# A ConvNet-and-experts layer: convolution by banded kernel matrices on TensorE, experts only on their own rows

## The chip, the cores and the metric

The kernel runs on one core of a Trainium2 chip. The metric is the device time of one execution in microseconds, median of the runs. All data is float32; matmuls are fp32 or f32r (float32 in TensorE's reduced form).

## The reference, cut to what matters

```python
r = relu((LN(x) @ w_reduce - mean) * gamma / sqrt(var + BN_EPS) + beta)   # 4x56x56, 128 -> 32
kgen = (r @ w_span + b_span).reshape(B, H, W, 16, 49)       # a 7x7 kernel per pixel and group
conv = einsum('bhwgk,bhwkgc->bhwgc', kgen, patches(LN(x)))  # 16 groups of 8 channels
t = x + conv
probs = softmax(LN(t) @ gate_w + gate_b)                    # 8 experts
cw = top two of probs, the others 0
out = t + sum_e cw[:, e] * (gelu(LN(t) @ W1[e] + b1[e]) @ W2[e] + b2[e])   # 128 -> 256 -> 128
```

There are 12,544 rows (pixels). Every expert is summed, but six of the eight weights of a row are zero.

## The kernel before

A row group is four image rows of two of the four images: 112 partitions (56 columns x 2 images) by four rows. There are 28 such groups (`q` and `bo`), each with eight steps `u` (an image row and half of the seven horizontal taps). All engines run the same loop `slot(q, bo)` in step order; later stages of earlier groups lie beside the convolution of the present one (`LAG_IN` = 14 steps later the first expert product, `LAG_OUT` 15, `LAG_WEIGH` 16, `LAG_ADD` 17).

Convolution: `kernels` makes on TensorE the kernels of 112 pixels, 4 or 3 horizontal taps at a time (L952). `products` on VectorE multiplies them with the normalised pixels over 3584 or 2688 elements (L744). POOL (`folds`, L434, L440) and, in two steps of eight, VectorE (`thin`, L750) add taps pairwise. `gather_taps` adds what is left on TensorE, by transposes that accumulate in one PSUM bank (L973). Two product tiles may lie between VectorE and TensorE.

Experts: for every group all eight experts are computed on all 448 rows. `expert_in` is three f32r matmuls of 448 columns for each half of the hidden layer (L1037 to L1039), `gelus` on ScalarE (L631), `expert_out` 8 fp32 matmuls (L1050), `weigh` on ScalarE scales by the row's weight `cw` (L621) and `add_expert` on VectorE sums (L764). SP only loads and stores; POOL also has the pow of the normalisations (L408) and the low part of the features `rT` (L421). Nothing is sorted and no DMA is indirect.

## Time and profile before

| | |
|---|---|
| runs | 1304.63, 1304.9, 1310.25 us; median 1304.9 |
| profiled execution, span of its core | 1302.3 us |
| VectorE, TensorE, POOL, ScalarE busy | 95%, 89%, 78%, 72% |
| mean granted TensorE clock | 0.954 |

The profiled execution's own time is its span and what lies around it; the three runs' median is 2.6 us over the span. A row of the profile gives line, engine, operation, output <- inputs with their tile names, and the shapes. An fp32 matmul that is no transpose leaves two records, each with its own weight load (engine PEld). Idle time in brackets names what ended it.

### The profile page before, as it was taken

The page shows a single profiled execution, that of the slowest core. Times are in us where ns is not written, and L with a number is a line of the kernel's source. Part 1 is how long each engine was busy: PE and PEld are TensorE (multiplying, and loading weights), DVE is VectorE, ACT ScalarE, POOL GpSimd, SP SyncE. Part 2 cuts the span into 40 slices and gives each one's busy share as a digit, 9 for nine tenths or more (in the row PEclk, how much of TensorE's full clock was granted, in tenths as well). Part 3 has the DMA queues.
Part 4 walks back from the last instruction along what each step waited for, and adds up shares of the span by engine and source line. Part 5 has one row for each costly group of instructions (what it writes and reads, how often), then busy time and mean ns, then how long its engine had stood idle before and what let it go on. Part 6 is the DMA issues. An engine that isn't in the chain of part 4 may idle for free. (4 is left out here: it accounts for less than half of the span.)

```text
span 1302.3 us, 27229 instructions
## 1 busy us (share of the span) xinstructions
PE 1154.1 (89%) x8857; PEld 1081.4 (83%) x8857; DVE 1237.1 (95%) x1222; ACT 941.2 (72%) x2975; POOL 1016.6 (78%) x558
## 2 busy tenths in 40 slices
PE   3999988999898889989888988898898889998987
PEld 3898888888788878889887888798888878888987
DVE  7789999999999999999999999999999999999942
ACT  3478877776777778777767777787777677667676
POOL 3248888988898898889888988988898889888830
PEclk9899999989999999889999999999999999899999
DMA  4100111011001101100110011011001100000000
GB/s 120 30 22 2 29 30 30 2 28 28 11 18 28 29 0 29 29 25 4 29 28 8 21 28 29 0 29 29 22 7 29 28 8 15 22 15 2 15 8 15
DMA packets 50007, 28.74 MB, mean 22 GB/s; under 512 B 6106, under 2 KB 46906, under 8 KB 49916
## 3 DMA queue, kind: packets, MB, share of 16 engines
q1 hardware_dynamic: 49892, 27.78, 7.8%
q8 instruction: 26, 0.43, 0.1%
q14 instruction: 65, 0.53, 0.1%
q10 hardware_dynamic: 24, 0.00, 0.0%
HBM read 15.38 MB, written 6.42 MB: 17 GB/s over the span
## 5 line engine op out<-in xcount | busy, mean ns | idle before, releaser
L744 DVE TENSOR_TENSOR prod<-kg,xn 112x3584 f32<-112x3584 f32 x224 | 762.0, 3414 | 9.2 <-PE kg L952 7.8
L434 POOL TENSOR_TENSOR prod<-prod 112x1536 f32<-112x1536 f32 x208 | 656.3, 3155 | 144.6 <-DVE prod L744 124.4
L1050 PE MATMUL y<-w_t,hT 128*112 128x128 f32 x3584 | 446.2, 279 | 0.0
L1050 PEld LDWEIGHTS y<-w_t,hT 128*112 128x112 f32 x3584 | 426.6, 184 | 2.1
L621 ACT ACTIVATE weighed<-y,cw 112x128 f32<-112x128 f32 x784 | 224.4, 373 | 140.1 <-DVE cw L837 104.0
L973 PE MATMUL conv<-ident,prod 112*128 112x112 f32 x2472 | 303.0, 276 | 0.0
L973 PEld LDWEIGHTS conv<-ident,prod 112*128 112x128 f32 x2472 | 279.8, 151 | 22.9 <-issue 12.7
L631 ACT ACTIVATE hT<-h,b_t 128x448 f32<-128x448 f32 x448 | 266.9, 657 | 43.0 <-PE h L1039 42.5
L440 POOL TENSOR_TENSOR prod<-prod 112x512 f32<-112x512 f32 (+1 forms) x182 | 249.3, 1370 | 14.3
L764 DVE TENSOR_TENSOR acc<-weighed,acc 112x512 f32<-112x512 f32 x168 | 180.7, 1076 | 18.8 <-ACT weighed L621 18.8
L1037 PE MATMUL h<-tn_hi,w_hi 128*128 128x448 f32 x448 | 182.2, 407 | 16.4 <-ACT hT L631 16.4
L1039 PE MATMUL h<-tn_hi,w_lo 128*128 128x448 f32 x448 | 167.8, 374 | 0.0
L1038 PE MATMUL h<-tn_lo,w_hi 128*128 128x448 f32 x448 | 167.2, 373 | 0.0
L952 PE MATMUL kg<-wk,rT 98*112 98x112 f32 x784 | 123.6, 275 | 22.4 <-DVE prod L744 19.5
L952 PEld LDWEIGHTS kg<-wk,rT 98*112 98x112 f32 x784 | 98.9, 182 | 27.1 <-DVE prod L744 22.7
L1037 PEld LDWEIGHTS h<-tn_hi,w_hi 128*128 128x128 f32 x448 | 85.9, 192 | 25.7 <-ACT hT L631 19.7
L408 POOL TENSOR_TENSOR rs<-ve,minus_half 112x4 f32<-112x4 f32 x53 | 64.1, 1210 | 51.1 <-ACT ve L519 51.1
L505 ACT ACTIVATE unread<-t_row 112x128 f32<-112x128 f32 x112 | 33.3, 298 | 84.9 <-DVE t_row L774 84.9
L1039 PEld LDWEIGHTS h<-tn_hi,w_lo 128*128 128x128 f32 x448 | 85.9, 192 | 7.9
L1038 PEld LDWEIGHTS h<-tn_lo,w_hi 128*128 128x128 f32 x448 | 86.0, 192 | 3.8
L750 DVE TENSOR_TENSOR prod<-prod 112x384 f32<-112x384 f32 (+1 forms) x52 | 78.9, 1517 | 0.0
L1018 PE MATMUL misc<-ident,cw 112*96 112x112 f32 x28 | 9.6, 341 | 57.6 <-DVE cw L837 57.6
(99 smaller groups left out, 1125.3 us busy)
## 6 DMA issues: line engine op xcount, KB each, us to landing
x_res<-in_x_dram SPq DMA_DIRECT2D x56, 112.0 KB
out_dram<-acc SPq DMA_DIRECT2D x56, 112.0 KB
x_in<-in_x_dram SPq DMA_DIRECT2D x54, 112.0 KB
stage<-xn SPq DMA_DIRECT2D x26, 224.0 KB, 2.7
w_raw<-in_L_ffn_W_dram SPq DMA_DIRECT2D x1, 1024.0 KB, 5.5
w_t<-in_L_ffn_W_dram SPq DMA_DIRECT2D x2, 512.0 KB, 6.3
prod<-in_L_conv_w_span_dram SPq DMA_DIRECT2D x3, 98.0 KB
prod<-in_x_dram SPq DMA_DIRECT2D x2, 112.0 KB
```

The lines of the kernel that those rows point to most:

```text
L434: nc.gpsimd.tensor_tensor(rows[:, :, 0:3 * C], rows[:, :, 0:3 * C], rows[:, :, 3 * C:6 * C], ALU.add).then_inc(fold_step if u in DEEP else ...
L440: nc.gpsimd.tensor_tensor(rows[:, :, 0:C], rows[:, :, 0:C], rows[:, :, tap * C:(tap + 1) * C], ALU.add).then_inc(folds_done, 1)
L621: ins = act.activation(to[0:T, rows], y_bank[e % 2][0:T, rows], ACT.Copy, scale=cw[bo][0:T, r * E + e:r * E + e + 1])
L631: act.activation(hT[e % 2][f][:, :], h_bank[f][:, 0:N], ACT.Gelu, bias=b1_t[:, 2 * e + f:2 * e + f + 1]).then_inc(gelu_done, 1)
L744: nc.vector.tensor_tensor(po, ks, xs, ALU.mult).then_inc(prod_done, 1)
L764: nc.vector.tensor_tensor(acc[bo][0:T, :], (y_bank if e == B2_WITH else weighed)[e % 2][0:T, :], (t_row if e == 0 else acc[bo])[0:T, :], A ...
L952: mm = pe.matmul(kg_bank[half][0:T, (j - j0) * K * G:(j - j0 + 1) * K * G], shifted(rT[bo], r, j), wk[:, j * K * G:(j + 1) * K * G], start ...
L973: mm = pe.matmul(shifted(conv_bank, r, j), prod[u % 4][0:T, at:at + C], ident_row, is_transpose=True, start=(u == 0 and j == j0 and i == 0 ...
L1037: pe.matmul(to, w1_hi[:, at], tn_hi[bo][:, :], start=True, stop=False)
L1038: pe.matmul(to, w1_hi[:, at], tn_lo[bo][:, :], start=False, stop=False)
L1039: pe.matmul(to, w1_lo[:, at], tn_hi[bo][:, :], start=False, stop=True).then_inc(h_ready, 1)
L1050: mm = pe.matmul(y_bank[e % 2][0:T, r * C:(r + 1) * C], hT[e % 2][f][:, r * T:(r + 1) * T], w2_t[:, (2 * e + f) * C:(2 * e + f + 1) * C], ...
```

## The change

Nearly the whole program is new; the reference's arithmetic is the same.

**Layout.** The image is cut into seven passes of eight rows. A pass has 16 steps: four quads (32 channels, four groups) times four strips (two rows). The normalised image is written to DRAM (`xpad`, `put_xn`), 28 DMAs for four image rows, such that `load_window` can fetch for a strip a window tile: 112 partitions are the 14 x 8 neighbourhood of a patch, the free side is image, patch column and 64 channels.

**Convolution.** A patch is two rows by eight columns, 16 positions. `kernels` makes for each group and position the kernels of 112 patches as a 112-row column in the neighbourhood's coordinates: the span weights lie in a wider zero image `wk`, and a shifted slice of it gives the band (L1065). `take_kernels` copies a bank of four positions to the ring `kb`, 12 of 16 on ScalarE and 4 on VectorE. `apply` contracts: for each patch one fp32 matmul, weights the window's 32 channels, moving the 64 columns (four groups by 16 positions) of `kb`, which stand 448 bytes apart; the four images' outputs go to four strips of 32 partitions (L1100). Of the four group blocks one holds for each channel; `take_conv` on VectorE zeroes the others, `turn_back` adds the four by accumulating transposes (L1110), `add_back` adds to the residual `t_row`.

**Experts.** The router takes the two largest, counts rows per expert by a scan and two matmuls (`ranks`, `rank`, `places`), and gives every (row, choice) a position in a list sorted by expert, padded to tiles of 128: 35 tiles a pass. `scatter` writes rows there by 32 indirect DMAs on POOL's queue; SP loads tiles; `stage` on VectorE reads the tile's expert number into a register and copies that expert's 642 columns of weights; `first_product`, gelu, `second_product`, `put_y` follow; 32 indirect `gather` DMAs fetch the results and `mix` on VectorE adds them by their weights. Pass n's expert slots stand in steps 10 of pass n+1 to 9 of pass n+2, two or three a step (`slots_at`), so the program ends with 48 steps without convolution. `requests_made` makes POOL wait for all its DMAs ahead of each of its other jobs. The loops are unrolled; no hardware loop is left.

```diff
-                nc.vector.tensor_tensor(po, ks, xs, ALU.mult).then_inc(prod_done, 1)
...
-                nc.gpsimd.tensor_tensor(rows[:, :, 0:3 * C], rows[:, :, 0:3 * C], rows[:, :, 3 * C:6 * C],
-                                        ALU.add).then_inc(fold_step if u in DEEP else folds_done, 1)
...
-                        mm = pe.matmul(shifted(conv_bank, r, j), prod[u % 4][0:T, at:at + C],
-                                       ident_row, is_transpose=True,
-                                       start=(u == 0 and j == j0 and i == 0),
-                                       stop=(u == STEPS - 1 and j == K - 1 and i == kept[-1]),
...
-                    pe.matmul(to, w1_hi[:, at], tn_hi[bo][:, :], start=True, stop=False)
-                    pe.matmul(to, w1_hi[:, at], tn_lo[bo][:, :], start=False, stop=False)
-                    pe.matmul(to, w1_lo[:, at], tn_hi[bo][:, :], start=False, stop=True).then_inc(h_ready, 1)
...
-                        mm = pe.matmul(y_bank[e % 2][0:T, r * C:(r + 1) * C], hT[e % 2][f][:, r * T:(r + 1) * T],
-                                       w2_t[:, (2 * e + f) * C:(2 * e + f + 1) * C], start=(r == 0 and f == 0),
-                                       stop=(f == 1), skip_group_check=True)
...
-                    ins = act.activation(to[0:T, rows], y_bank[e % 2][0:T, rows], ACT.Copy,
-                                         scale=cw[bo][0:T, r * E + e:r * E + e + 1])
...
-                nc.vector.tensor_tensor(acc[bo][0:T, :], (y_bank if e == B2_WITH else weighed)[e % 2][0:T, :],
-                                        (t_row if e == 0 else acc[bo])[0:T, :], ALU.add).then_inc(acc_done, 1)
...
+    START = 10
+    SLOTS = NT + 1
+    PER_STEP = [2, 2, 2, 3]
...
+        n, o = divmod(t - STEPS - START, STEPS)
+        if not 0 <= n < NC:
+            return []
+        first = sum(PER_STEP[(START + k) % 4] for k in range(o))
+        return [(n, first + k) for k in range(PER_STEP[(START + o) % 4])]
...
+            def put_xn(u):
+                sp.wait_ge(xn_ready, u + 1)
+                for half in range(2):
+                    for hh in range(2):
+                        for pw in range(PW):
+                            w0, w1 = max(0, 8 * pw - 3), min(W, 8 * pw + 11)
+                            row = 4 * u + 2 * hh + 3
+                            j0 = w0 + 3 - 8 * pw
+                            to = xpad[half, j0:j0 + w1 - w0, row:row + 2, :]
+                            to = to.rearrange("j r (b p c) -> j (r b) p c", b=B, p=PW)[:, :, pw, :]
+                            sp.dma_start(to, cols(xs[u % 2], 0, 8)[hh * W + w0:hh * W + w1, :, half * 64:half * 64 + 64]) \
+                                .then_inc(xn_out[u % 2], 16)
...
+            def load_window(n, half, s):
...
+                sp.dma_start(win[k % WSLOTS][:, :],
+                             xpad[half, :, row:row + 8, :].rearrange("j r f -> j (r f)")) \
+                    .then_inc(win_loaded[k % WSLOTS], 16)
...
+            got_count = [0] * 8
+            def requests_made():
+                if count["scattered"]:
+                    pool.wait_ge(scattered, count["scattered"])
+                for slot in range(8):
+                    if got_count[slot]:
+                        pool.wait_ge(got_row[slot], got_count[slot])
...
+            def rstd2(v):
+                requests_made()
+                pool.wait_ge(ve2_ready, v + 1)
+                if v:
+                    pool.wait_ge(tn_ready, v)
+                nc.gpsimd.tensor_tensor(rs2[:, :], ve2[:, :], minus_half[0:T, :], ALU.pow).then_inc(pow2_done, 1)
+                pool.wait_ge(pow2_done, v + 1)
+                nc.gpsimd.tensor_tensor(nb2[:, :], nm2[:, :], rs2[:, :], ALU.mult).then_inc(rstd2_ready, 1)
+                pool.wait_ge(rstd2_ready, v + 1)
...
+            def scatter(n, i):
...
+                pool.indirect_dma_start(xrows[n % 2], bass.IndirectOffsetOnAxis(ap=pos[n % 2][:, i:i + 1], axis=0),
+                                        tn[:, c * C:(c + 1) * C], None) \
+                    .then_inc(scattered, 16)
...
+            def gather(n, i):
...
+                if use >= 8:
+                    pool.wait_ge(mixed, use - 8 + 1)
+                pool.indirect_dma_start(got[:, slot * C:(slot + 1) * C], None, yrows[n % 2],
+                                        bass.IndirectOffsetOnAxis(ap=pos[n % 2][:, k * COLS + c:k * COLS + c + 1], axis=0)) \
+                    .then_inc(got_row[slot], 16)
...
+            def take_kernels(Q, j):
...
+                act.wait_ge(kg_done, bank_no + 1)
+                if g >= GSLOTS:
+                    act.wait_ge(main_done, 4 * ((g - GSLOTS) // 4 + 1))
...
+                act.activation(kb[:, lo:lo + 4 * PATCHES], kg_bank[j % 2][0:WIN, 0:4 * PATCHES], ACT.Copy) \
+                    .then_inc(kb_act, 1)
...
+            def take_conv(t):
...
+                dve.wait_ge(main_done, t + 1)
...
+                nc.vector.tensor_tensor(conv[t % 2][:, :].rearrange("p (g k) -> p g k", g=4),
+                                        e_bank[t % 2][:, 0:4 * T].rearrange("p (g k) -> p g k", g=4),
+                                        group_mask[:, turn:turn + 4].unsqueeze(2).to_broadcast([128, 4, T]),
+                                        ALU.mult).then_inc(conv_ready, 1)
...
+            def stage(n, i):
+                m = NT * n + i
+                if i == 0:
+                    dve.wait_ge(soft_step, SOFT * n + 31)
+                if m >= 3:
+                    dve.wait_ge(y_out, m - 2)
+                at = dve.value_load(te[n % 2][0:1, i:i + 1], min_val=0, max_val=(E - 1) * ROW)
+                dve.tensor_copy(staged[(NT * n + i) % 3][:, :], table[:, bass.ds(at, ROW)]).then_inc(weights_in, 1)
...
+            def put_y(n, i):
...
+                at = slice((i % 4) * C, (i % 4 + 1) * C)
+                nc.vector.tensor_tensor(yo[g % 2][:, at], xy_bank[:, at], staged[(NT * n + i) % 3][:, 2 * HID + 2:ROW], ALU.add) \
+                    .then_inc(y_out, 1)
...
+            def mix(n, i):
...
+                to = t_row[n % 3][:, c * C:(c + 1) * C]
+                dve.scalar_tensor_tensor(out=to, in0=got[:, (i % 8) * C:(i % 8 + 1) * C],
+                                         scalar=wt[n % 2][:, k * COLS + c:k * COLS + c + 1], in1=to,
+                                         op0=ALU.mult, op1=ALU.add).then_inc(mixed, 1)
...
+            def kernels(Q, j):
...
+                r = rT[n % 2][:, :].rearrange("p (u r k b) -> p u r k b", u=2, r=2, b=8)[:, :, a, :, :]
+                for i in range(4):
+                    at = g * IMG + 57 - 8 * (b4 + i) - a
+                    mm = pe.matmul(kg_bank[j % 2][0:WIN, i * PATCHES:(i + 1) * PATCHES], wk[:, at:at + WIN],
+                                   r[:, :, :, b4 + i], start=True, stop=True, skip_group_check=True)
+                mm.then_inc(kg_done, 1)
...
+            def apply(t, pw):
...
+                    to = e_bank[t % 2][32 * b:32 * b + 32, 0:4 * T]
+                    to = to.rearrange("p (g a w c) -> p g a w c", g=4, a=2, c=8)[:, :, :, pw, :]
+                    at = (b * PW + pw) * 64 + (q % 2) * 32
+                    mm = pe.matmul(to, w[:, at:at + 32], rhs, start=True, stop=True, skip_group_check=True)
+                if pw == PW - 1:
+                    mm.then_inc(main_done, 1)
...
+            def turn_back(t):
...
+                for x_ in range(4):
+                    mm = pe.matmul(back[0:T, s * 128:(s + 1) * 128], conv[t % 2][:, x_ * T:(x_ + 1) * T], ident[:, :],
+                                   is_transpose=True, start=(x_ == 0), stop=(x_ == 3), skip_group_check=True)
+                mm.then_inc(back_done, 1)
...
+            def first_product(n, i):
...
+                pe.wait_ge(weights_in, m + 1)
+                pe.wait_ge(xT_ready, GROUPS * n + i // 4 + 1)
+                if m:
+                    pe.wait_ge(gelu_done, m)
...
+                for f in range(2):
+                    mm = pe.matmul(h_bank[:, f * 128:(f + 1) * 128], staged[(NT * n + i) % 3][:, f * 128:(f + 1) * 128],
+                                   xT[:, at:at + 128], start=True, stop=True, skip_group_check=True)
+                mm.then_inc(h_done, 1)
...
+            def second_product(n, i):
...
+                pe.wait_ge(gelu_done, m + 1)
+                if m:
+                    pe.wait_ge(y_out, m - 1 if i % 4 == 3 else m)
+                pe.wait_ge(xT_ready, GROUPS * n + min(GROUPS, i // 4 + (2 if i % 4 >= 2 else 1)))
...
+                for f in range(2):
+                    mm = pe.matmul(xy_bank[:, at], hT[(NT * n + i) % 2][:, f * 128:(f + 1) * 128],
+                                   staged[(NT * n + i) % 3][:, HID + f * C:HID + (f + 1) * C], start=(f == 0), stop=(f == 1),
+                                   skip_group_check=True)
+                mm.then_inc(y_done, 1)
...
+            def expert_slot(n, i):
+                for k in tiles_out(i):
+                    second_product(n, k)
+                if i == 0:
+                    turn_rows(n, 0)
+                if i % 4 == 3 and i // 4 + 1 < GROUPS:
+                    turn_rows(n, i // 4 + 1)
+                if i < NT:
+                    first_product(n, i)
...
+                if live:
+                    apply_wait(t)
+                    for pw in range(PW):
+                        apply(t, pw)
+                        if pw == 1 and more:
+                            kernels(Q + 1, 2 * s)
+                        if pw == 3 and s:
+                            turn_back(t - 1)
+                        if pw == 4 and more:
+                            kernels(Q + 1, 2 * s + 1)
+                    if s == 3:
+                        turn_back(t)
...
+                work = slots_at(t)
+                if live and s == 3 and more:
+                    for j in range(8, 16):
+                        kernels(Q + 1, j)
+                        if j % 2 and (j - 9) // 2 < len(work):
+                            expert_slot(*work[(j - 9) // 2])
+                else:
+                    for m, i in work:
+                        expert_slot(m, i)
```

TensorE, steady middle. Before: parts of two steps, `h` and `y` the expert products, `conv` the taps.

```order
L973 MATMUL conv<-ident,prod 128x112 x9
L1050 MATMUL y<-w_t,hT 112x128 x8
L952 MATMUL kg<-wk,rT 112x112 x3
L1037 MATMUL h<-tn_hi,w_hi 128x448
L1038 MATMUL h<-tn_lo,w_hi 128x448
L1039 MATMUL h<-tn_hi,w_lo 128x448
L1037 MATMUL h<-tn_hi,w_hi 128x448
L1038 MATMUL h<-tn_lo,w_hi 128x448
L1039 MATMUL h<-tn_hi,w_lo 128x448
L989 MATMUL misc<-ident,convT 112x128 x4
```

After, the last step of a quad (numbers of buffers shown; `e` is apply's bank, `kg` the kernels', `back` and `misc` the turns', `xy` an expert tile's).

```order
L1100 MATMUL e1<-kb,win2 32x8x8 x8
L1065 MATMUL kg0<-rT1,wk 112x112 x4
L1100 MATMUL e1<-kb,win2 32x8x8 x8
L1110 MATMUL back<-ident,conv0 112x128 x4
L1100 MATMUL e1<-kb,win2 32x8x8 x4
L1065 MATMUL kg1<-rT1,wk 112x112 x4
L1100 MATMUL e1<-kb,win2 32x8x8 x8
L1110 MATMUL back<-ident,conv1 112x128 x4
L1045 MATMUL misc<-ident,xs1 128x112 x4
L1065 MATMUL kg0<-rT1,wk 112x112 x4
L1065 MATMUL kg1<-rT1,wk 112x112 x4
L1177 MATMUL xy<-staged0,hT1 128x128 x2
```

The conv transposes and 448-column products are gone; apply matmuls stand between kernels, and single tiles' products between them.

VectorE, steady middle, before:

```order
L744 TENSOR_TENSOR prod<-kg,xn 112x3584
L755 REGISTER_ALU
L764 TENSOR_TENSOR acc<-weighed,acc 112x512
L750 TENSOR_TENSOR prod<-prod 112x4x128
L736 REGISTER_ALU
L744 TENSOR_TENSOR prod<-kg,xn 112x2688
L755 REGISTER_ALU
L764 TENSOR_TENSOR acc<-weighed,acc 112x512
L779 TENSOR_TENSOR tn_lo<-misc,tn_hi 128x448
```

After, where a pass's router work begins (`yo` is put_y, TENSOR_LOAD and COPY are stage):

```order
L910 TENSOR_TENSOR yo0<-xy,staged0 128x128
L900 TENSOR_LOAD te0
L900 ISA x2
L901 ISA
L901 COPY staged0<-table 128x642
L771 TENSOR_TENSOR conv1<-e1,group_mask 128x448
L829 TENSOR_REDUCE m1<-ex2 112x16
L831 TENSOR_TENSOR eq<-ex2,m1 112x128
```

The products are gone; each tile brings an addition, a register load and a 642-column copy.

POOL, before, where the pow of a normalisation stands among the folds:

```order
L440 TENSOR_TENSOR prod<-prod 112x4x128
L405 ISA
L407 REGISTER_ALU
L408 TENSOR_TENSOR rs<-ve,minus_half 112x4
L410 TENSOR_TENSOR nb<-nm,rs 112x4
L433 REGISTER_ALU
L434 TENSOR_TENSOR prod<-prod 112x3x384
```

Both kinds wait for VectorE or ScalarE only. After, the same engine while a pass's rows are scattered:

```order
L488 TENSOR_TENSOR nb<-nm,rs 112x8
L508 TENSOR_TENSOR rT<-r_lin,rT 32x448
L518 DMA xrows<-tn,pos 4480x128 x10
L508 TENSOR_TENSOR rT<-r_lin,rT 32x448
L518 DMA xrows<-tn,pos 4480x128 x11
L508 TENSOR_TENSOR rT<-r_lin,rT 32x448
L518 DMA xrows<-tn,pos 4480x128 x5
```

The folds are gone, and the small jobs on which TensorE's next pass rests stand behind scatters.

## Rows read from the trace of the kernel before

**Rows 1.** Page, busy time: us, share of the span, instructions.
```profile
PE 1154.1 (89%) x8857; PEld 1081.4 (83%) x8857; DVE 1237.1 (95%) x1222; ACT 941.2 (72%) x2975; POOL 1016.6 (78%) x558
```

**Rows 2.** Steady middle: length; busy us of PE, PEld, DVE, ACT, POOL; clock; DMA share.
```profile
650.00:741.00 91.00, 81.42 (x627) 75.64 (x626) 90.54 (x85) 68.57 (x221) 78.04 (x41) 0.96 0.07 21
```

**Rows 3.** Groups by shape: busy us, mean ns, idle before; products and y.
```profile
L1050 PE MATMUL y<-w_t,hT 128*112 128x128 f32 x3584 | 446.2, 279 | 0.0
L744 DVE TENSOR_TENSOR prod<-kg,xn 112x3584 f32<-112x3584 f32 x112 | 434.4, 3879 | 2.1 <-PE kg L952 1.5
...
L744 DVE TENSOR_TENSOR prod<-kg,xn 112x2688 f32<-112x2688 f32 x112 | 330.4, 2950 | 7.1 <-PE kg L952 6.3
```

**Rows 4.** Timeline of TensorE: start us, length us, merged count at the end.
```profile
644.47 1.91 PE L1050 MATMUL y<-w_t,hT 128*112 128x128 f32 x16
646.54 0.58 PE L952 MATMUL kg<-wk,rT 98*112 98x112 f32 x4
...
652.77 0.24 PE L1008 MATMUL misc<-gate_parts,tn_hi 128*112 128x16 f32 x1
652.87 0.24 PE L1010 MATMUL misc<-gate_parts,tn_lo 128*112 128x8 f32 x1
...
45.48 2.88 PE L973 MATMUL conv<-ident,prod 112*128 112x112 f32 x28
```

**Rows 5.** Groups by shape: weight loads of 128, 112 and 96 columns.
```profile
L1037 PEld LDWEIGHTS h<-tn_hi,w_hi 128*128 128x128 f32 x448 | 85.9, 192 | 25.7 <-ACT hT L631 19.7
...
L952 PEld LDWEIGHTS kg<-wk,rT 98*112 98x112 f32 x784 | 98.9, 182 | 27.1 <-DVE prod L744 22.7 <-issue 4.2
...
L939 PEld LDWEIGHTS misc<-xnT,wred 128*96 128x96 f32 x56 | 9.1, 169 | 7.2 <-ACT xnT L550 4.5 <-issue 1.0
```

**Rows 6.** Groups by shape: VectorE's strided and contiguous CAST.
```profile
L888 DVE CAST wk<-prod 98x112 fp32r<-98x112 f32 x7 | 1.8, 330 | 0.0
...
L898 DVE CAST wk<-wk_lo 32x784 fp32r<-32x784 f32 x1 | 0.6, 558 | 0.0
```

**Rows 7.** Timeline of ScalarE: start us, length us, merged count.
```profile
685.12 1.13 ACT L621 ACTIVATE weighed<-y,cw 112x128 f32<-112x128 f32 x4
686.12 1.18 ACT L631 ACTIVATE hT<-h,b_t 128x448 f32<-128x448 f32 x2
687.16 1.67 ACT L581 ACTIVATE tn<-t_row,nb,rs 112x128 f32<-112x128 f32 x4
...
33.81 0.54 ACT L550 ACTIVATE xnT<-misc 128x448 f32<-128x448 f32 x1
```

**Rows 8.** Groups by shape: VectorE on 448 columns from PSUM, and a small operation.
```profile
L779 DVE TENSOR_TENSOR tn_lo<-misc,tn_hi 128x448 fp32r<-128x448 f32 x28 | 17.1, 612 | 0.8 <-ACT tn_hi L590 0.8
...
L802 DVE TENSOR_TENSOR logits_part<-misc,gate_bias 112x32 f32<-112x32 f32 x28 | 4.9, 176 | 2.4 <-PE misc L1010 2.4
```

**Rows 9.** Groups by shape: POOL's pow and its 448-column subtraction.
```profile
L408 POOL TENSOR_TENSOR rs<-ve,minus_half 112x4 f32<-112x4 f32 x53 | 64.1, 1210 | 51.1 <-ACT ve L519 51.1
...
L421 POOL TENSOR_TENSOR rT<-r_lin,rT 32x448 fp32r<-32x448 f32 x28 | 27.3, 976 | 13.1 <-ACT r_lin L563 9.3 <-POOL prod L434 3.5
```

**Rows 10.** Timeline of the head: statistics on VectorE, DMA issues on SP.
```profile
4.51 0.87 DVE L715 BATCH_NORM_STATS2 prod<-x_in 112x6 f32<-112x128 f32 x4 [4.51 <-DMA x_in<-in_x_dram]
...
17.97 4.01 SPq L333 DMA_DIRECT2D w_t<-in_L_ffn_W_dram  x2
22.02 4.65 SPq L339 DMA_DIRECT2D b_raw<-in_L_ffn_b_dram  x12
```

**Rows 11.** DMA issues: count, KB each, us from issue to landing.
```profile
stage<-xn SPq DMA_DIRECT2D x26, 224.0 KB, 2.7
w_raw<-in_L_ffn_W_dram SPq DMA_DIRECT2D x1, 1024.0 KB, 5.5
```

**Rows 12.** Page, DMA queue: packets, MB, share of 16 engines' span.
```profile
q1 hardware_dynamic: 49892, 27.78, 7.8%
```

1738 lines of the change are left out of this document (892 added, 846 removed).

## The prediction

> **What bounds the kernel now.** I read the busy shares first, then a stretch of the steady middle, then the costliest groups. VectorE is busy 95% of the span [rows 1]; in 91 us of the middle, which is two of the 28 row groups, it is busy 90.5 us while TensorE's granted clock is 0.96 of full [rows 2]. So the time is VectorE's work: 45.5 us a row group x 28 = 1274 us, and a head and a tail. Most of it is the product of kernels and pixels, 224 instructions of 3.9 and 2.95 us [rows 3]. TensorE is busy 89% of the span [rows 1], nearly a second bound. A change has to take work from both. This one throws VectorE's products away, puts the convolution on TensorE and cuts the experts' work there. Nothing of the old loop is left, so the new time is a sum of its own, not a difference.
>
> **Units of the sum.** The new program makes seven passes of eight image rows; a pass has 16 steps. On TensorE what counts is the pace, not the length of a record. Where a row merges k matmuls, pace = (its length - 0.28)/(k-1), 0.28 us being one matmul's own length. An fp32 matmul leaves two records (3584 of them for the 1792 y matmuls [rows 3]), a transpose or an f32r one leaves one. Paces: fp32 over 128 columns (1.91-0.28)/15 = 0.109 us a record; a kernels matmul (0.58-0.28)/3 = 0.100; a transpose over 112 columns (2.88-0.28)/27 = 0.096; a gate matmul that moves 16 or 8 columns starts 0.10 after the one before [rows 4]. Streamed columns thus cost 0.85 ns each; the load of 96, 112, 128 weight columns takes 169, 182, 192 ns [rows 5], 0.7 to 0.8 ns a column.
>
> **TensorE's work in one pass.**
> Experts: 35 tiles of 128 rows, each one transpose (0.11) and four fp32 matmuls (8 x 0.109 = 0.87): 35 x 0.98 = 34 us. Before, two expert products of all eight experts took the larger part of the engine.
> Kernels: 64 banks x 4 = 256 matmuls x 0.10 = 26 us.
> Back-transposes: 64 x 0.11 = 7 us. Other turns, reduction (8 records x 448 columns x 0.85 ns = 3.1) and gate (32 x 0.10): 32 x 0.096 + 3.1 + 3.2 = 9 us.
> Apply: 448 fp32 matmuls with 32 weight columns and 64 moving ones. **This price is in no row.** If every record waits its turn it streams 64 x 0.85 = 0.055 us, 0.11 a matmul. If issuing is the limit, the smallest pace shown stands, 0.096 a record, 0.19 a matmul. If the four consecutive matmuls, which write four separate strips of 32 partitions, run beside each other, the floor is the weight load, 32 x 0.85 = 0.028 a record, 0.055 a matmul or even less. I take 0.055: the two records of one matmul must follow each other in their strip, but the next matmul's can overlap them. 448 x 0.055 = 25 us. Ends: 20 (a pass; beyond the weight load no row gives a reason) and 86 us.
> Here TensorE's rows have no case of separate strips. The Trainium skill (TensorE: Matmul & The Clock Gate, Part 3) has three tiles of 32 columns, N = 512, running 2.38 times as fast as one after another; by it an estimate of 0.11/2.38 = 0.046 us a matmul, 28 us less in the whole kernel, and no run here shows it.
> Sum of work: 34 + 26 + 7 + 9 + 25 = 101 us.
>
> **TensorE's waits in one pass.** A handoff is 0.1 us, a matmul's tail 0.17. Gelu over 448 columns paces at 0.59, a 128-column ACTIVATE at 0.28, so I take 0.65 for a tile's pair; a 448-column copy is 0.55 [rows 7].
> In 12 of 16 steps two expert slots stand back to back: the second waits 0.17 + 0.1 + 0.65 + 0.1 = 1.0 us for the first's gelu: 12 us. Nine groups wait for their transposed rows, 0.9 each: 8 us.
> At each fourth step the ring of kernel slots forces eight banks behind the last apply: a wait for the masked copy on VectorE (448 columns, 0.61 [rows 8]) 1.0, for the last bank's copy 0.9, and the alternation of TensorE (5.8 us of work) with ScalarE (six copies, three pairs, 5.3 us) over two banks, taken at 2.5: 4 x 4.4 = 18 us.
> The router: four copies 3.6, nine small VectorE operations before the rank matmul at about 0.25 (0.18 [rows 8] and a semaphore) 2.3, and 4 for the normalisation chain: 10 us.
> Sum: 48 us; the ends are 30, if the alternation and the normalisation chain vanish and half the gelu waits do, and 75, if each wait is half as long again. **A pass is 101 + 48 = 149 us.**
>
> **What hides under it.** VectorE: 16 masked copies x 0.61, 16 bank copies x 0.55, 8 additions x 0.4, four moment sets x 2.4 (eight statistics pace at 0.22 [rows 10]), 31 router operations x 0.25, 35 x (weights copy 0.5, register load 0.7, bias add 0.22), 32 mixes x 0.22: about 96 us. The register load is in no row; VectorE hides it up to 2.2 us a tile, then VectorE is the bound. ScalarE: 48 copies, 32 normalisations at 0.41, 35 gelu pairs, 25 other copies: 80 us. The price of a plain weights copy comes from 558 ns for 784 columns [rows 6].
> POOL: 64 indirect DMAs. No row has one. SP's issues are 0.39 us each for the smallest and 2.0 for 1024 pieces [rows 10]; I take 1.2, the length of POOL's pow [rows 9], to keep to its software pace. 64 x 1.2 + 6 + 4 + eight drains of 2.7 (a landing [rows 11]) = 109 us, hidden; at 2.0 it would be 160, no longer hidden.
> DMA: about 192,000 small packets against 49,892 in 7.8% of the span [rows 12], four times as many, plus 45 MB of windows. 1024 KB landed in 5.5 us [rows 11], so 56 windows of 0.8 MB are 240 us of transfer. Hidden.
>
> **Head and tail.** Head: SP issues three sets of 28 padded writes and 18 zero fills before the window of step 2: 102 x 0.5 (between 0.39 and 2.0, nearer the small ones) + 15 others, + 5.5 to land = 72 us, less 8 of steps 0 and 1: 64 us. Passes: 7 x 149 = 1043, less 26 steps without experts (34 + 12 + 8 + 4 in 16 steps): 94, so 949. Tail, after the last apply: router chain beside nine slots 30; 32 scatters x 1.2 and a landing 41; 36 slots at 1.9 (two products 0.9, gelu 0.65, handoffs and tails 0.35) plus nine turns at 0.9, with the load, 79; store, 32 gathers x 1.2, output 45: 195 us. Span 64 + 949 + 195 = 1208; with the 2.6 us by which the median stands over the profiled span (1304.9 - 1302.3), **1211 us**.
>
> **Rivals.**
> A, strips do not overlap: a matmul costs 0.11, a pass 174, total 1211 + 3136 x 0.055 = **1383 us, slower**. The deciding point is (1305 - 1211)/3136 = 0.030 above my price: at 0.085 us an apply matmul the change is worth nothing. For it: in every row the paces are those of one matmul behind another. Against: all of these fill at least 96 weight columns.
> B, strided reads cost: the apply's moving operand steps 448 bytes, that of the kernels 32; all of TensorE's moving operands now are contiguous. VectorE's strided CAST of 112 columns takes 330 ns, 1.6 ns a column above its fixed 150, against 0.52 in the contiguous one [rows 6]. With 1.6 ns a column on TensorE, kernels 0.18 and apply 0.102 even with overlap: +143 +148 = **1502 us**. Against: TensorE's fp32 pace of 0.85 ns leaves room that VectorE's 0.52 does not.
> The Trainium skill (SBUF — State Buffer, Door 1) speaks against the change here: 16-byte lines, two hits needed for full rate. It would have the effect of B; the strided CAST agrees in kind.
> C, POOL's requests cost 2.0 us: a pass 160, +66 over the six passes that have them, +51 in the tail: **1328 us**. For it: 448 requests on an engine that needs 1.2 us for four powers. At 0.39 only the tail gains: 1159.
> D, the waits come out at 75 instead of 48, because in-order engines lag behind each other: **1400 us**; at 30: **1085**.
> That the change doesn't do what it says is excluded: the new order has 3136 apply matmuls and no product on VectorE.
>
> **Chances.** Overlap and waits roughly as counted 0.45 (own range 1120 to 1290); cheaper waits or apply 0.12; A 0.20; B 0.10; C or D 0.13. The first two lie under 1298, with a sliver of the first at no change. Within 0.5%, which is what a measurement of this kernel can tell from no change: 0.05. Faster 0.56, slower 0.39. The range 1100 to 1480 holds all but B and the far ends.
>
> **What would show it.** The apply line's merged rows: 28 matmuls (56 records) in 1.6 us if right, 3.1 under A, 6 under B without overlap. Kernels rows: four in 0.58 if strides are free, 0.85 under B. TensorE near 65 to 70% busy and VectorE at 60%, with the chain through TensorE and ScalarE. Waits of TensorE on the gelu of about 1 us, some 80 of them. Under C TensorE and ScalarE wait for POOL's rs and rT. A tail of some 200 us with TensorE mostly idle. The prediction is wrong first if apply costs over 0.085 us, next if another engine's lag adds more than 14 us to a pass.

## The result and the profile after

The changed kernel takes 1636.6 us (four runs, 1618.7 to 1646.7) against 1305.1 before: a ratio of 1.249, 95% interval 1.242 to 1.256. It is 25% slower. The prediction was 1211 us and faster, its range ended at 1480. Its profiled run, the fastest of the four, has a span of 1616.9 us and a mean granted clock of 0.718; the slowest has 0.668.

From the page after: span, busy time of each engine, the granted clock in 40 slices, and two DMA queues. They answer to [rows 1] and [rows 12].

```profile
span 1616.9 us, 30101 instructions
PE 1183.4 (73%) x11249; PEld 965.4 (60%) x11249; DVE 548.5 (34%) x1694; ACT 533.9 (33%) x1246; POOL 522.8 (32%) x566
PEclk9999655566797665966557967569565797577795
q1 hardware_dynamic: 169080, 116.41, 30.0%
q0 software_dynamic: 14336, 25.72, 5.7%
```

VectorE went from 1237 us of work to 549, so the old bound is gone. TensorE is now the busiest engine, at 73%. What is new is the clock row: before, the clock was 0.954 in the mean, 0.96 in [rows 2]; now 30 of the 36 slices behind the head are at 5 to 7 tenths. The trace's record of the clock has 121 us at the lower of the two levels (1.2 GHz) before, 914 us after.

One steady pass of the after kernel, as busy times of each engine, with clock and DMA share; it answers to [rows 2]:

```profile
core 0: us, PE busy (x) PEld busy (x) DVE busy (x) ACT busy (x) POOL busy (x), PEclk, DMA share, GB/s
695.00:904.50 209.50, 168.88 (x1547) 140.10 (x1550) 75.70 (x232) 74.38 (x176) 73.33 (x76) 0.63 0.37 90
```

VectorE, ScalarE and GpSimd have 73 to 76 us of work in 209; none is a bound. What the clock does to a price is seen in one stretch of TensorE's timeline (start, length, line, tiles, shapes, how many merged, idle time before and what ended it). It answers to [rows 4]:

```profile
762.15 0.63 PE L1100 MATMUL e<-kb,win 112*32 112x64 f32 x16
762.71 0.63 PE L1065 MATMUL kg<-rT,wk 98*112 98x112 f32 x4
763.27 0.63 PE L1100 MATMUL e<-kb,win 112*32 112x64 f32 x16
763.83 0.65 PE L1110 MATMUL back<-ident,conv 128*112 128x128 f32 x4
...
765.87 0.71 PE L1177 MATMUL xy<-staged,hT 128*128 128x128 f32 x4
766.41 0.61 PE L1165 MATMUL h<-xT,staged 128*128 128x128 f32 x4
770.36 1.19 PE L1177 MATMUL xy<-staged,hT 128*128 128x128 f32 x4 [3.34 <-issue]
771.34 1.06 PE L1165 MATMUL h<-xT,staged 128*128 128x128 f32 x4
772.34 0.66 PE L1100 MATMUL e<-kb,win 112*32 112x64 f32 x16
772.92 1.00 PE L1065 MATMUL kg<-rT,wk 98*112 98x112 f32 x4
...
774.43 1.10 PE L1110 MATMUL back<-ident,conv 128*112 128x128 f32 x4
```

Up to 767 the level is full; TensorE then waits 3.3 us, and behind the wait the same rows take 1.00 for 0.63 (kernels), 1.10 for 0.65 (back), 1.06 for 0.61 (experts). Start to start over the whole trace: a kernels matmul 99 ns at the full level and 187 at the low one, an expert record 112 and 213, a transpose back 109 and 214. Only the apply rows do not change, 0.63 and 0.66: sixteen of their records start in 0.56 to 0.58 us at either level, 0.035 us a record, 0.070 a matmul.

With these prices a pass can be split three ways: what the low level adds to the records that ran at it; starts that come over 0.5 us behind the one before (waits); the rest, which is work at the full level. The split is an estimate, worked out from the starts in the traces; another way of drawing the lines moves a term by up to 10 us. Figures are us, for the pass that begins near the given time.

| kernel, pass from | length | low level adds | waits | work at full level |
|---|---|---|---|---|
| forecast | 149 | 0 | 48 | 101 |
| after, 800 | 209 | 37 | 54 | 118 |
| after, 1009 | 207 | 38 | 50 | 119 |
| e9_again, 653 | 263 | 58 | 85 | 120 |
| k13_again, 644 | 266 | 63 | 87 | 117 |
| e5_noind, 754 | 198 | 34 | 46 | 118 |
| e12_noind_fill, 723 | 178 | 10 | 22 | 146 (118 and 28 of fills) |
| m18_all, 627 | 232 | 20 | 74 | 138 (118 and 20 of fills) |

The work column is the same 118 wherever the work is the same. From the first strip at 67 us to the last at 1377 the after kernel spends 771 us of work, 323 of waits, 216 on the low level; the forecast for that stretch was 949 = 652 + 297 + 0 (seven passes of 101 and 48, less 55 and 39 for 26 steps without experts).

### The profile page after: what moved, and what is told of

It reads as the page before. It is cut to its first block and busy times, and to the rows that moved or that the text cites. A ratio compares the mean times of both kernels' runs of the same rounds, so it can differ in the third digit from the quotient of the medians.

```text
span 1616.9 us, 30101 instructions
## 1 busy us (share of the span) xinstructions
PE 1183.4 (73%) x11249; PEld 965.4 (60%) x11249; DVE 548.5 (34%) x1694; ACT 533.9 (33%) x1246; POOL 522.8 (32%) x566
## 3 DMA queue, kind: packets, MB, share of 16 engines
q1 hardware_dynamic: 169080, 116.41, 30.0%
## 5 line engine op out<-in xcount | busy, mean ns | idle before, releaser
L1065 PE MATMUL kg<-rT,wk 98*112 98x112 f32 x1792 | 349.7, 350 | 4.5 <-POOL rT L508 2.9
L1065 PEld LDWEIGHTS kg<-rT,wk 98*112 98x112 f32 x1792 | 300.6, 250 | 48.6 <-issue 39.3
L533 POOL DMA_INDIRECT got<-yrows,pos x224 | 212.1, 947 | 309.2 <-DVE t_row L922 191.7
L1177 PE MATMUL xy<-staged,hT 128*128 128x128 f32 x980 | 207.3, 360 | 115.7 <-ACT hT L654 43.8
L1100 PE MATMUL e<-kb,win 112*32 112x64 f32 x6272 | 257.7, 294 | 21.9 <-ACT kb L613 21.0
L518 POOL DMA_INDIRECT xrows<-tn,pos x224 | 215.9, 964 | 142.3 <-DVE pos L883 75.1
L1177 PEld LDWEIGHTS xy<-staged,hT 128*128 128x128 f32 x980 | 169.5, 252 | 146.1 <-ACT hT L654 102.2
L613 ACT ACTIVATE kb<-kg 112x448 f32<-112x448 f32 x336 | 178.4, 545 | 234.2 <-PE kg L1065 232.5
L1165 PE MATMUL h<-xT,staged 128*128 128x128 f32 x980 | 205.5, 348 | 40.1 <-ACT hT L654 32.9
L1165 PEld LDWEIGHTS h<-xT,staged 128*128 128x128 f32 x980 | 179.2, 257 | 49.1 <-issue 42.8
L1100 PEld LDWEIGHTS e<-kb,win 112*32 112x32 f32 x6272 | 153.7, 134 | 89.9 <-issue 33.2
L1110 PE MATMUL back<-ident,conv 128*112 128x128 f32 x448 | 100.3, 364 | 28.3 <-DVE conv L771 28.3
L1154 PE MATMUL xy<-ident,xin 128*128 128x128 f32 x245 | 55.6, 368 | 84.9 <-DMA xin<-xrows 60.2
L1110 PEld LDWEIGHTS back<-ident,conv 128*112 128x112 f32 x448 | 62.9, 172 | 51.3 <-DVE conv L771 35.5
```

Of the source, the lines that this page charges most:

```text
L518: pool.indirect_dma_start(xrows[n % 2], bass.IndirectOffsetOnAxis(ap=pos[n % 2][:, i:i + 1], axis=0), tn[:, c * C:(c + 1) * C], None) \
L533: pool.indirect_dma_start(got[:, slot * C:(slot + 1) * C], None, yrows[n % 2], bass.IndirectOffsetOnAxis(ap=pos[n % 2][:, k * COLS + c:k * ...
L613: act.activation(kb[:, lo:lo + 4 * PATCHES], kg_bank[j % 2][0:WIN, 0:4 * PATCHES], ACT.Copy) \
L1065: mm = pe.matmul(kg_bank[j % 2][0:WIN, i * PATCHES:(i + 1) * PATCHES], wk[:, at:at + WIN], r[:, :, :, b4 + i], start=True, stop=True, skip ...
L1100: mm = pe.matmul(to, w[:, at:at + 32], rhs, start=True, stop=True, skip_group_check=True)
L1110: mm = pe.matmul(back[0:T, s * 128:(s + 1) * 128], conv[t % 2][:, x_ * T:(x_ + 1) * T], ident[:, :], is_transpose=True, start=(x_ == 0), s ...
```

## The experiments

**Theory 1**: the waits of TensorE let its granted clock fall, and the low level is what costs. **Theory 2**: the waits alone cost, the clock follows. **Theory 3**: the strip matmuls, with 32 weight columns each where the others have 96 to 128, are what lowers the clock. "Stops" below are starts over 0.48 us behind the one before inside a row of matmuls of one line; matmuls of 448 columns, which take longer than that at the low level by themselves, are left out. After's own profile has 3, and for all three it names the engine or the DMA that TensorE waited for. The kernel before took 1304.4 to 1306 us beside every one of these.

**e1_fill.** Ahead of every second product, and of the other waits:

```diff
+            def fill(count):
+                for _ in range(count):
+                    pe.matmul(e_bank[(now[0] + 1) % 2][:, 0:128], ident[:, :], ident[:, :], start=True, stop=True,
+                              skip_group_check=True)
...
             def second_product(n, i):
                 m = NT * n + i
+                fill(4)
```

> The changed kernel with some 230 matmuls of 128 columns a pass added that nobody reads, four (eight at the ranks) ahead of each wait that TensorE's trace shows: gelu, xT, tnT, the conv mask at a fourth step, the last kernel copies. They take 0.11 us each at the full level, so 25 us a pass if nothing hides them. Theory 1 (short waits let the granted clock fall, and the low level is what costs): the waits are still there, but TensorE works in them, so the clock rises from 0.72 to over 0.80 and the time falls by 80 to 250 us, to 1390 to 1560, although work is added. Theory 2 (the waits themselves and the queue order cost, the clock is a bystander): nothing to gain; 1640 to 1800, clock unchanged. Theory 3 (the strip matmuls of 32 columns in four quadrants are what the clock falls under): clock unchanged at 0.72, 1640 to 1800.

1953.5 us, clock 0.803, 143 stops. The clock rose as theory 1 wants, the time did not fall as it wants: the run lies above all three ranges. The price of a fill was also wrong, two records of 0.112, so 52 us a pass, 364 in seven passes.

**e2_early.** `part(o - 4, 6, ...)` in steps 4 to 9 becomes `part(o - 4, 4, ...)` in steps 4 to 7:

> The 32 scatters of a pass are asked for in steps 4 to 7 and not 4 to 9, so that none stands behind GpSimd's wait for the features of step 7. Theory 2 (waits): the stall of TensorE for xin, 8 to 19 us once a pass, goes: 60 to 100 us less, 1540 to 1580, clock within 0.03 of 0.72. Theory 1 (clock): the same stall goes and with it one fall of the clock a pass: 80 to 160 us less. If the rows are late for another reason (the scatters' landing, the load), under 20 us of change.

1962.7 us, clock 0.620, 160 stops: 326 us slower than the after kernel's own 1637 for the same instructions in another order on one queue. No theory had this. The timelines of GpSimd, ScalarE, VectorE, SyncE's queue and TensorE in one stretch:

```profile
730.15 1.03 POOL L518 DMA_INDIRECT xrows<-tn,pos  x1 [0.29 <-POOL rT L508]
731.49 0.95 POOL L518 DMA_INDIRECT xrows<-tn,pos  x1 [0.30 <-issue]
...
749.05 0.94 POOL L518 DMA_INDIRECT xrows<-tn,pos  x1 [0.30 <-issue]
```

```profile
735.09 0.54 ACT L613 ACTIVATE kb<-kg 112x448 f32<-112x448 f32 x1 [2.77 <-remote]
750.02 0.54 ACT L613 ACTIVATE kb<-kg 112x448 f32<-112x448 f32 x1 [14.38 <-issue]
```

```profile
733.19 0.50 DVE L901 COPY staged<-table 128x642 f32 x1 [0.30 <-issue]
752.95 0.62 DVE L771 TENSOR_TENSOR conv<-e,group_mask 128x448 f32<-128x448 f32 x1 [19.26 <-remote]
```

```profile
732.26 21.48 SPq L317 DMA_DIRECT2D win<-xpad  x2
```

```profile
737.23 0.41 PE L1100 MATMUL e<-kb,win 112*32 112x64 f32 x4 [1.01 <-issue]
738.66 0.40 PE L1100 MATMUL e<-kb,win 112*32 112x64 f32 x4 [1.02 <-issue]
```

GpSimd sends sixteen requests one behind the other, 1.245 us each with the gap. Some 5 us into the run ScalarE starts nothing for 14.4 us, though the kernels that it copies are there at 735.4; VectorE waits 19.3 us; SyncE's two window loads, issued in 3.9 us in the after kernel, take 21.5; TensorE goes on in pieces of a few matmuls with 0.3 to 1 us between, for which the profile names no engine. When the sixteenth request is out, at 750.0, ScalarE starts in the same moment. This became **theory 4**: a run of indirect requests holds up all other engines.

**e3_noexp** (no expert slots, gathers or mixing) and **e4_thin** (4 of 28 strip matmuls a step):

> Leaves out all expert slots (loads, turns, both products, gelu, staging, stores), the gathers and the mixing; router and scatters stay. Theory 1: TensorE has no gelu and xT waits, so the clock is at 0.88 or more in all seven passes as in the first pass of the trace (129.9 us, 24.5 us of it at the low level): 67 + 7 x 130 + 40, about 1020 us (980 to 1060). Theory 3 (the strips lower the clock): clock near 0.72 without experts too, passes of 150 to 165, 1150 to 1260.

1224.8 us, clock 0.638, 114 stops: far over the 1020, so the experts' waits are not all of it. The time lies in theory 3's range, but that range knew nothing of the stops.

> From the third step on, applies only the last of the seven window positions: 4 of 28 strip matmuls a step, 24 left out, no added waits. By the traced pace of 0.070 us for one these are 1.7 us a step and 188 us in 112 steps. Theory 2: 150 to 190 us less (1445 to 1490), clock the same or lower, since busy time goes and the waits stay. Theory 3: the clock rises to over 0.85 and 350 us or more go. Theory 1: clock the same or lower; the kernels' evictions wait more, so under 190 us less, 1440 to 1560.

1683.0 us, clock 0.618, 37 stops. The strips that are left out are worth 188 us by their own pace. With six in seven gone the clock did not rise: against theory 3. The time lies outside all three ranges. The low count of stops says little here, since the long rows of one line in which they are counted are gone: ScalarE and VectorE together still start nothing for up to 15 us while requests are out.

**e5_noind.** No scatters and no gathers:

```diff
-                if 4 <= o < 10 and 0 <= n - 1 < NC:
+                if False:
...
-                if o >= 10 and 0 <= n - 2 < NC:
+                if False:
...
-                dve.scalar_tensor_tensor(out=to, in0=got[:, (i % 8) * C:(i % 8 + 1) * C],
+                dve.scalar_tensor_tensor(out=to, in0=table[0:T, c * C:(c + 1) * C],
```

> Leaves out all 64 indirect DMAs of a pass (32 scatters, 32 gathers) and nothing else: the experts' rows stay zero, the mixing reads the weight table, all products, copies, other transfers and additions are kept. Theory 4, new after the first four runs (a long run of indirect requests on GpSimd holds up the other engines and SyncE's queue: in the run with early scatters ScalarE, VectorE and SyncE start nothing for 14 to 20 us until GpSimd's sixteenth request is out, TensorE goes on in pieces of 0.7 us; these waits then pull the clock down): no such holds, passes of 145 to 165 instead of 206, clock over 0.80, 1180 to 1320 us in all. Theory 1 (gelu, xT and conv waits pull the clock down without any help from the requests): only the wait for xin goes, 8 us a pass; 1540 to 1600, clock 0.70 to 0.75.

1524.7 us (1.167, interval 1.163 to 1.171), clock 0.714, 5 stops. For all five the profile names whom TensorE waited for, so the unexplained stops are gone. The low clock is not gone: 871 us at the low level. The time lies between the two ranges, 15 us under theory 1's, whose clock it has. Neither theory alone.

**e6_nogather, e7_four, e8_early_four.** The gathers alone left out; and, on after and on e2, `if i % 4 == 0: requests_made()` ahead of each scatter and gather, `requests_made` being the wait for the rows of all open requests.

> Leaves out the 32 gathers of a pass, keeps the scatters; the mixing reads the weight table. Theory 4: half the requests and about half of what the run without any gains, 1380 to 1500; the holds left lie in the scatters' stretch. Theory 1: within 2% of 1637.

1815.1 us, 127 stops.

> The same work; GpSimd waits for the rows of all its open requests before each fourth request, so no run is longer than four (5 us). GpSimd's queue gets 12 to 14 waits of 2.4 us more a pass, 30 us, which are beside other work. Theory 4: the holds go although nothing is left out: 1350 to 1560 and a clock over 0.75. Theory 1: the same or slower, 1620 to 1700, since the scatters end later and xin is waited for longer.

1816.4 us, clock 0.640, 38 stops.

> Scatters in steps 4 to 7 as in the run that took 1963 us, but in runs of four at most with a wait for the rows before the next. Theory 4: the 320 us that the early scatters cost go, and the wait for xin too: 1330 to 1550. If it is their place and not the length of the run that cost 320 us: 1900 to 2000.

1798.2 us, clock 0.624, 40 stops. All three lie outside every range given for them. Read against 1637 all three got slower with less work or the same, so the changed kernel itself was measured again.

**e9_again, k13_again.** No edit; measured on two chips.

> The changed kernel once more, unchanged, beside the next three and on their chip. Seven of the eight runs so far, two with less work in them among them, had 37 to 160 stops of TensorE over 0.48 us inside a row of matmuls of one line, 44 to 175 us together, which the changed kernel's own profile has not (3 stops, 2.4 us). If these stops come from the edits, this run gives 1620 to 1650 us again and under 10 stops. If they come with the chip or the hour, it gives 1750 to 1950 and 50 stops or more, and the earlier runs have to be read against this one.

1932.9 us (1.481, 1.472 to 1.489), clock 0.639, 138 stops.

> The changed kernel unchanged, the control of this call. If the time of 1637 us or 1933 us goes with the chip, it is one of the two or between them, and its profile has under 10 or over 100 stops of TensorE inside a line's row accordingly.

1944.6 us (1.492, 1.483 to 1.502), clock 0.606, 140 stops. The page of e9_again, the busy row and the clock:

```profile
span 1925.6 us, 30101 instructions
PE 1314.0 (68%) x11249; PEld 1062.3 (55%) x11249; DVE 550.7 (29%) x1694; ACT 537.9 (28%) x1246; POOL 522.3 (27%) x566
PEclk9986565676665556755666666666656596656675
```

So the same program has been seen at 1637 us with 3 stops and, on two chips, at 1933 and 1945 with 140. Its 448 requests are no slower, 953 ns against 955; what changed is whether they stop the others. The profile names whom TensorE waited for in only 5 of e9_again's 138 stops; of the other 133, 112 fall while a run of requests is out, which is 30% of the span. The kernel before has no such request and did not move. The experiments from e1 on that keep requests all show stops and are read against these two runs: e1 and e2 came out 1% above them, e1 with 52 us of fills a pass, e6 without its gathers 6% below, and e7 and e8 6 to 7% below. A run without requests (e5, e11, e12, m19) cannot show which condition it had, and each was measured on another chip than some of those it is compared with. Shorter runs of requests help, as theory 4 says, by less than its ranges. Leaving all of them out is worth 1939 - 1525 = 414 us, 0.92 us a request, about the length of the request itself (against the first measurement it would be 112 us, 0.25 a request); in the convolution alone (e3 against e11, below) 200 us for 224 requests, 0.89 each.

**e10_spread.** In steps that end in two expert slots, the first one moves behind window position 3 on TensorE, between the two kernel copies on ScalarE, ahead of the mask copy on VectorE:

```diff
                         if pw == 3 and s:
                             turn_back(t - 1)
+                        if pw == 3:
+                            for m_, i_ in early_slot(t):
+                                expert_slot(m_, i_)
```

> Where a step has two expert slots at its end, the first is moved between the window positions of the same step's convolution, on all engines, so that the gelu of one lies beside the strips and kernels and not ahead of the next slot's product. The same work. Twelve waits of 1.2 us a pass go, 14 us. Theory 1: the clock's falls that these waits bring go too, the low level falls from 57% to under 45% of the span: 150 to 250 us less than the unchanged kernel of the same call. If the clock falls for other reasons: 60 to 100 us less and the same clock.

1799.9 us (1.378), clock 0.666: 133 us under its control. The low level's time fell from 1391 us to 1203. The twelve gelu waits a pass were put at 14 us, 98 in seven passes, so the gain is somewhat more than their length. It lies between the two ranges, and the stops fell as well, from 138 to 101, so the clock's part in it is not separated.

**e11_conv.** Neither experts nor any indirect DMA:

> Leaves out all expert slots, gathers, mixing and scatters: convolution, norms and router only, no indirect DMA. The run that still had the scatters took 1225 us with 114 stops. Theory 4: all stops go, passes of 126 to 130 and a clock over 0.85: 1000 to 1060 us. If strips and kernels stop on their own: passes of 145 or more, 1120 to 1230.

1025.1 us, in the range, but with a clock of 0.631 where over 0.85 was expected. It has 12 stops, and for each the profile names whom TensorE waited for (VectorE 6, ScalarE 5, a DMA 1), so the unexplained stops went with the requests, as theory 4 says. Two passes in turn take 132 and 141 us, 91 and 121 of them at the low level, with only 19 us of TensorE idle: in the convolution alone the clock is low with few waits, which theory 1 does not explain.

**e12_noind_fill.** e5 with `fill(3)` ahead of 33 waits a pass (the second slot of a step, xT, tnT, the mask at a fourth step, the last kernel copies):

> As the run without indirect DMAs (1524.7 us, clock 0.714, 5 stops: the same parts left out), with three matmuls of 128 columns that nobody reads ahead of 33 waits a pass (the gelu between two slots, xT, tnT, the mask copy at a fourth step, the last kernel copies). Each takes 0.22 us at the full level, two records of 0.112, so 0.67 at a place that waits 0.6 to 1.3: 22 us a pass, nearly all of it inside the waits. (The first fill run had 52 us a pass, not the 25 that its expectation reckoned with.) Theory 1: the low level's time falls by half or more, clock over 0.85, 1330 to 1450 us although work is added. If waits are not what the clock falls for: 1530 to 1620 and clock 0.68 to 0.75.

1420.4 us (1.085, 1.078 to 1.092) against e5's 1524.7, with 28 us of work added to a pass. The clock rows of e5 and of e12:

```profile
PEclk9968657967596565875668766659656667857777
```

```profile
PEclk9995565589799987999979999799987899979997
```

The low level's time fell from 871 us to 397, the mean clock rose from 0.714 to 0.862. Nothing was taken away, only matmuls were added ahead of waits, and 104 us went: in the passes with experts the added matmuls raise the clock, and that pays. Two limits. The fills are also full-width matmuls, and no run put them anywhere else, so it is not shown that it is the filled wait and not the added work that holds the clock up. And in the first pass, which has no experts, they did nothing: 98 of 143 us at the low level, against 70 of 127 in e5 and 25 to 79 in the unchanged kernel's three profiles. In the table above a steady pass loses 24 us of low level and 24 of waits for 28 of fills, so on their own the fills were paid by the waits that they lie in, and the clock is the gain. The Trainium skill says of this (TensorE: Matmul & The Clock Gate, "HAM oscillation" and "A second HAM failure mode") that waits between groups of matmuls make the clock fall again and again, short ones too. The after kernel's trace agrees, with 0.63 in the pass from 695 us and some 54 us of waits in a pass; e11_conv has the low level with 19 us idle as well.

**k14_fill_few**, the same fills in the complete kernel, **k15_rows32** (`pos[...][0:32, ...]` and 32 rows of `tn` or `got` in each request) and **k16_nowin** (no `put_xn` from the fourth set on, no window load from the sixth), all beside k13_again:

> The complete changed kernel with the 33 fills a pass of three unread matmuls (22 us a pass, 0.22 us each). Theory 1 (waits pull the granted clock down): clock over 0.75 and 60 to 200 us less than this call's control, as 104 us went in the run without indirect DMAs. If the stops behind GpSimd's requests are all that counts: control plus 0 to 100 us.

1902.2 us against 1944.6 on the same chip, clock 0.749 against 0.606. The 42 us (2%) are clear of the noise, but under the 60 to 200 of theory 1, and not the loss of its rival: the fills raise the clock in the complete kernel too, and the gain is mostly paid back in fills.

> Each of the 64 indirect DMAs of a pass moves 32 of its 112 rows, the other rows are left out; as many requests, all else kept. If the stops come from what a request writes for each row, and its cost on GpSimd too, a request falls from 0.95 us to under 0.6 us, the longest silence of ScalarE and VectorE inside a run of requests falls under 3 us, and the time comes to 1520 to 1620 us, as without indirect DMAs. If they come with the request whatever its size: within 3% of this call's control.

1964.0 us, 144 stops against 140: within the 3% of "the request whatever its size". Of GpSimd's groups with 32 rows (busy, mean ns, idle before):

```profile
L534 POOL DMA_INDIRECT got<-yrows,pos x224 | 198.6, 887 | 509.6 <-DVE t_row L923 302.5 <-issue 154.0 <-DMA yrows<-yo 49.1
```

887 ns for 32 rows against 953 for 112 in k13_again: the request costs, not its rows, and it stops the others as often. The longest silence of ScalarE and VectorE together, 10.9 us against 25.5, is shorter, but not under 3.

> From the second pass on, leaves out the stores of normalised rows to the padded copy (28 transfers each) and the window loads, so TensorE works on the first five windows again; requests and all compute kept. These are about four in five of the packets of SyncE's queue. If the stops need both kinds of transfers side by side, they go: under 30 stops, 1500 to 1640 us. If GpSimd's requests stop the others alone: within 3% of this call's control.

1953.8 us, 155 stops, with q1's share of the span down to 13.2% from the 25.1% of k13_again and its bytes to 67 MB from 116. Its packets fell from 169,080 to 126,222, a quarter and not the four in five of the expectation. So the stops do not need that half of the other queue's traffic; whether they need the rest was not tried.

**m18_all and m19_wide.** All that helped together (scatters in steps 4 to 7, runs of two, e10's order, e12's fills); and e5 with seven matmuls of 128 weight columns a step:

> The complete kernel with all that helped: scatters asked for in steps 4 to 7, at most two indirect requests in a row before GpSimd waits for their rows, the first of two expert slots moved between the window positions, and three unread matmuls ahead of 33 waits a pass. Against the unchanged one at 1933 to 1945: early scatters with runs of four gave about 140 us, moved slots 133, fills 42. If they add up: 1600 to 1680 and a clock over 0.78, under 60 stops. If each took the same waits away: 1720 to 1800. In neither case under the 1305 us of before.

1822.8 us (1.393), clock 0.756, 12 stops: above both ranges. The stops went (for one alone the profile names nobody), but with a wait for each second request the scatters end late, and TensorE waits for `xin` once a pass, 169.5 us in 7 waits against 60.2 in the after kernel. The edits did not add up. No version that does the whole work beats the kernel before.

```diff
-                for b in range(B):
+                for b in range(1):
...
-                    to = e_bank[t % 2][32 * b:32 * b + 32, 0:4 * T]
+                    to = e_bank[t % 2][:, 0:4 * T]
...
-                    mm = pe.matmul(to, w[:, at:at + 32], rhs, start=True, stop=True, skip_group_check=True)
+                    mm = pe.matmul(to, w[:, at:at + 128], rhs, start=True, stop=True, skip_group_check=True)
```

> As the run without indirect DMAs (1524.7 us, clock 0.714, 871 us at the low level), but each step applies 7 matmuls of 128 weight columns over the whole array, those of image 0, in place of 28 strips of 32 columns; images 1 to 3 are left out. At the records' pace of 0.07 to 0.11 us these 14 records take 1.0 to 1.6 us against 1.96 for the strips. Theory 3 (the strips, which fill a quarter of the array's columns each, keep the clock low): clock over 0.82 and 1300 to 1420 us. Theory 1 (waits alone): clock 0.68 to 0.76; only the strips' shorter time goes, 0.4 to 1.0 us a step: 1410 to 1490.

1576.7 us (1.198); its two fastest runs, 1556 and 1572 us, have clocks of 0.719 and 0.723 against 0.695 to 0.721 in e5's four: the clock did not rise, the time did, by some 40 us. Above every range. The page's rows of the apply line in m19_wide and in e5_noind:

```profile
L1100 PE MATMUL e<-kb,win 112*128 112x64 f32 x1568 | 361.2, 370 | 19.8 <-ACT kb L614 18.4
```

```profile
L1100 PE MATMUL e<-kb,win 112*32 112x64 f32 x6272 | 258.1, 294 | 22.7 <-ACT kb L614 21.2
```

A quarter as many full-width matmuls start 0.111 us apart at the full level and 0.213 at the low one: 14 records, 1.6 or 3.0 us a step, where 28 strips take 1.96 at either. Theory 3 falls for the passes that make up the time. In the first pass, which has no experts, it may hold: there m19_wide had no low level at all in 140 us, against 70 of 127 in e5_noind, and every profile with strips has at least 24. So what raised the clock in one kind of pass (fills with experts, wide matmuls without) did nothing in the other, and what keeps it low while strips run with few waits was not settled.

## Why the prediction was wrong

Predicted 1211; 1617 in the profiled run, with what lies around it 1619. The differences by term: work between first and last strip 119, waits there 26, low level there 216, tail 44, head 3. They make 408.

- **The step that failed: every price at the full clock.** The paragraph on units took all paces from rows at the full level, most from the middle at 0.96 [rows 2, 4], and carried them over to a kernel whose TensorE waits 48 us in a pass of 149 by the forecast's own sum. No rival let the clock fall. Kernels, experts, back-transposes and turns, 76 of the 101 us, go by the clock. Low level in all: 240 us with the tail's 23. That is 59% of the miss. Without it the sum of this profile would be 1377 us, an estimate from the paces above, in the stated range but still 5% slower than before: the sign would have been wrong too, since the missing work alone (119 us) is more than the 94 us that were to be won.
- **Apply at 0.055 a matmul.** Measured 0.070: 1.96 us a step where 1.6 stood and 3.1 under rival A; 47 us in the whole kernel. The strips do overlap, as the forecast said: most of their records start 7 ns behind the one before. A is out by its own test (0.085 was its deciding point), although its 1383 is near the 1377 by accident. The estimate of 0.046 from the Trainium skill (TensorE: Matmul & The Clock Gate, Part 3) was further off than 0.055. How many times faster 0.070 is than one strip after another, no run shows: the forecast's 0.055 a record was itself an estimate, and the only 64-column matmuls measured by themselves, those of m19_wide with 128 weight columns, start 0.111 us a record apart.
- **The rest of the work**, 10 us a pass: 118 measured, less 7 for apply, against 101. The sum counted each group at its inner pace. A group of four kernels matmuls takes 0.56 us from its start to the next group's (762.71 to 763.27 above), four times 0.100 is 0.40; 64 such groups a pass are 10 us.
- **Strides (rival B)** cost nothing in the kernels matmuls, with their steps of 32 bytes: four 0.63 us at the full level with their own length in it, a start every 99 ns, against 99 in the kernel before where the operand was contiguous; 0.58 was foreseen and 0.85 under B. The rule on 16-byte lines of the Trainium skill (SBUF — State Buffer, Door 1), weighed in the prediction, does not show in these reads. The 448-byte steps of apply have no contiguous counterpart in any run.
- **Waits (rival D)**: 54 us a pass against 48, right. The parts, in the whole span: gelu waits 43.8 us in 58, xT 39.5 in 28, the mask 28.3 in 29, tnT 18.0 in 28. One was missing, the rows from DMA, because scatters of steps 8 and 9 stand on GpSimd's queue behind its wait for the features of step 7. (In e2_early, whose scatters stand in steps 4 to 7, this wait is 4.0 us in all, against 60.2 here and 35.7 in e9_again.)

```profile
engine line waited for: us in total, times, longest us
PE xy L1154 <- DMA xin<-xrows: 60.2, 7, 18.4
PE xy L1177 <- ACT hT L654: 43.8, 58, 1.3
PE xy L1177 <- ACT xT L660: 39.5, 28, 1.9
PE h L1165 <- ACT hT L654: 32.9, 10, 7.0
PE back L1110 <- DVE conv L771: 28.3, 29, 7.4
```

- **GpSimd (rival C)**: a request takes 0.95 to 0.96 us, under the 1.2 taken, 428 us in all, and GpSimd is busy 523 us; as a price it was safe. "Hidden" was wrong in kind: in the two later measurements its requests stopped the engines that were to hide them, and the same program took 300 us more (31 to 33 us of waits a pass, 21 to 26 of low level). The price of 0.95 does not show this, the silence of the others does.

```profile
L518 POOL DMA_INDIRECT xrows<-tn,pos x224 | 215.9, 964 | 142.3 <-DVE pos L883 75.1
L533 POOL DMA_INDIRECT got<-yrows,pos x224 | 212.1, 947 | 309.2 <-DVE t_row L922 191.7
L901 DVE COPY staged<-table 128x642 f32 x245 | 125.6, 513 | 136.2 <-DVE yo L910 115.4
L771 DVE TENSOR_TENSOR conv<-e,group_mask 128x448 f32<-128x448 f32 x112 | 69.8, 623 | 218.7 <-PE e L1100 218.6
```

- **VectorE and ScalarE** were hidden, as said: 76 and 74 us of work a pass against 96 and 80. The weights copy took 0.51 (0.5), the mask 0.62 (0.61).
- **Head** 67 us against 64, right. **Tail** 239 against 195, half of the difference the low level.
- **TensorE 65 to 70% busy**: 73%; **VectorE 60%**: 34%, because the work lies in a longer span and was 20 us a pass less.

What stays open: why the requests stop the others in one measurement and not in another; what distinguishes the first measurement is not known, nor on which chip it was made. By which path they do it was not found either; the number of rows and about half of the other queue's traffic are excluded. In the four profiles without any request (e5, e11, e12, m19) TensorE has no stop for which the profile names nobody, so nothing points to a second source. And what lowers the clock is shown in part only: that the low level cost 240 us is measured, that filled waits are what raises it in the passes with experts is argued from e12 and k14, and the convolution alone is not explained.

## What to carry to other kernels

If a change takes an engine from 89% busy with hardly a wait to a chain of short matmul groups with a wait between them, price its work at both clock levels and give the low one a rival of its own: here it was 240 of 408 us. One run with unread matmuls ahead of the waits shows how much of it can be had back. Before believing that work on GpSimd is hidden, look at what the others start while it runs, and when numbers taken at different times do not fit together, measure the unchanged kernel again beside them.
